# A softmax pipeline over five engines: four probability buffers, every engine's order shifted, five heads with the maximum as bias

## The reference

```python
q = hidden_state @ Wq + bq          # 32 heads of 16
k = encoder_hidden_state @ Wk + bk  # 8 heads of 16
v = encoder_hidden_state @ Wv + bv
scores = jnp.einsum('bkgld,bksd->bkgls', q, k) * scale + mask
attn = jax.nn.softmax(scores, axis=-1)
out = jnp.einsum('bkgls,bksd->bkgld', attn, v)   # then @ Wo + bo, + x, layer norm
```

## Time and profile before

| | |
|---|---|
| median of 3 runs | 2727.72 us |
| the profiled execution | 2733.99 us, span 2732.2 us |
| busy, share of the span | PE 90%, DVE 48%, POOL 33%, ACT 28% |
| mean granted TensorE clock | 0.955 |
| layer 0, first half, PT copy 0 to PT copy 31 | 49.02 to 222.77 us, 173.75 us |
| layer 0, second half, the same | 1410.14 to 1580.55 us, 170.41 us |

### The profile page before, as it was taken

One profiled execution on the slowest core, in us unless ns is written; L12 is line 12 of the kernel. 1 busy time (PEld: TensorE's weight loads), 2 busy tenths in 40 slices (PEclk: granted clock), 3 DMA queues, 4 the chain that ended last, 5 costly groups with the idle time before them and its releaser, 6 DMA issues.

```text
span 2732.2 us, 40539 instructions
## 1 busy us (share of the span) xinstructions
PE 2453.1 (90%) x14896; PEld 2086.6 (76%) x14896; DVE 1322.8 (48%) x2066; ACT 758.7 (28%) x2134; POOL 909.8 (33%) x568
## 2 busy tenths in 40 slices
PE   5776999999799999889966769999998999998898
PEld 4555888888688888767755558888886888886677
DVE  5767433333643333564467783433336333435544
ACT  4553222222222222211145522222222222222111
POOL 4663323222432223322146632322233222323221
PEclk8888999999999999999988889999999999999999
DMA  4001011010110101110130011111002101101000
GB/s 169 9 9 58 33 37 54 31 38 31 66 52 33 38 32 53 37 37 31 62 136 9 9 58 39 46 39 38 31 31 74 47 31 38 52 33 43 31 31 31
DMA packets 34532, 120.08 MB, mean 44 GB/s; under 512 B 3456, under 2 KB 3712, under 8 KB 33408
## 3 DMA queue, kind: packets, MB, share of 16 engines
q1 hardware_dynamic: 34432, 118.69, 12.2%
HBM read 114.48 MB, written 4.19 MB: 43 GB/s over the span
## 4 chain that ended last, share of the span: by engine, by line
PE 76%; DVE 8%; issue 6%; POOL 5%; ACT 2%; DMA 1%; SPq 0%; DVEq 0%; POOLq 0%; ACTq 0%
PE PS L449 63%; PE PS L659 4%; PE PS L641 4%; PE PS L650 2%; PE PS L517 2%; POOL X L316 1%; DVE MX L987 1%; POOL XN L336 1%; DMA BO<-in_bo_rows 1%; DVE XN L982 1%; PE PS L551 1%; DVE X L1006 1%; POOL W L303 1%; POOL XN L329 1%; DVE HF L1081 1%
## 5 line engine op out<-in xcount | busy, mean ns | idle before, releaser
L449 PE MATMUL PS<-AT,W 128*128 128x512 f32 x2496 | 607.5, 395 | 24.9 <-DVE HF L1081 12.1
L449 PEld LDWEIGHTS PS<-AT,W 128*128 128x128 f32 x2496 | 473.1, 190 | 129.7 <-issue 13.4
L1006 DVE TENSOR_TENSOR X<-PS,X 128x512 f32<-128x512 f32 x416 | 284.3, 689 | 334.5 <-PE PS L449 327.2
L390 POOL TENSOR_TENSOR PR<-PR,RC 128x512 f32<-128x512 f32 x128 | 133.6, 1044 | 932.6 <-DVE RC L1171 932.6
L449 PE MATMUL PS<-W,CX 128*128 128x512 f32 x1584 | 397.3, 404 | 34.5 <-DVE Q L974 25.5
L449 PE MATMUL PS<-CT,W 128*128 128x512 f32 x1584 | 399.7, 401 | 30.6 <-DVE W L303 25.7
L449 PE MATMUL PS<-W,CT 128*128 128x256 f32 (+1 forms) x3264 | 412.1, 287 | 0.0
L449 PEld LDWEIGHTS PS<-W,CT 128*128 128x128 f32 x3264 | 401.6, 195 | 0.6
L449 PEld LDWEIGHTS PS<-W,CX 128*128 128x128 f32 x1584 | 294.1, 190 | 105.9 <-DVE Q L974 27.1
L449 PEld LDWEIGHTS PS<-CT,W 128*128 128x128 f32 x1584 | 290.6, 190 | 88.8 <-DVE W L303 26.1
L310 POOL TENSOR_SCALAR W<-RAW 128x1024 fp32r<-128x1024 f32 (+1 forms) x136 | 154.2, 1134 | 554.0 <-PE PS L449 531.7
(11 more groups left out here) (92 smaller groups left out, 2540.5 us busy)
## 6 DMA issues: line engine op xcount, KB each, us to landing
RAW<-in_wq SPq DMA_DIRECT2D x44, 512.0 KB, 4.1
RAW<-in_wo SPq DMA_DIRECT2D x44, 512.0 KB, 3.3
RAW<-in_wk SPq DMA_DIRECT2D x40, 512.0 KB, 3.3
RAW<-in_wv SPq DMA_DIRECT2D x40, 512.0 KB, 3.3
X<-in_x SPq DMA_DIRECT2D x2, 2048.0 KB, 10.0
BVR<-in_bv_rows SPq DMA_DIRECT2D x8, 512.0 KB, 4.2
BIASVR<-in_biasv_rows SPq DMA_DIRECT2D x8, 512.0 KB, 5.7
out<-X SPq DMA_DIRECT2D x4, 1024.0 KB, 4.4
```

The lines of the kernel that those rows point to most:

```text
L390: nc.gpsimd.tensor_tensor(PR[:, :, 0:P], PR[:, :, 0:P], RC[:, 0, 0:BT].unsqueeze(2).to_broadcast([P, BT, P]), ALU.mult).then_inc(norm_done, 1)
L449: ins = nc.tensor.matmul(out, lhs(c, a), rhs(c, b), start=(k == 0), stop=(k == total - 1))
L1006: V_.tensor_tensor(X[:, tile, :], PS[:, bank, :], X[:, tile, :], ALU.add).then_inc(done, 1)
```

## The change

```diff
@@ constants
-OWN = 3
+OWN = 5
+BUFS0 = 4
@@ build: MX, arena and the fourth buffer
-        MX = sb("MX", [P, 3, 8])
+        MX = sb("MX", [P, BUFS0, 8])
...
-        ARENA = 45056
+        ARENA = 49152
...
+        P0D = in_arena("P0D", [P, 1024], F32, 45056)
+
         P0 = [XN[:, 0:2, :].rearrange("p a n -> p (a n)"), XN[:, 2:4, :].rearrange("p a n -> p (a n)"),
-              HF[:].rearrange("p a n -> p (a n)")]
+              HF[:].rearrange("p a n -> p (a n)"), P0D[:]]
@@ gpsimd: order of the turns
                 sub(0)
                 sub(1)
                 norm(0)
+                sub(2)
                 for s in range(STEPS0):
-                    if s + 2 < STEPS0:
-                        sub(s + 2)
                     if s + 1 < STEPS0:
                         norm(s + 1)
+                    if s + 3 < STEPS0:
+                        sub(s + 3)
@@ tensor: order of the turns
                 s0_(1)
                 s0_(2)
+                s0_(3)
                 for s in range(STEPS0):
                     t0(s)
                     if s:
                         pv0(s - 1)
-                    if s + 3 < STEPS0:
-                        s0_(s + 3)
+                    if s + 4 < STEPS0:
+                        s0_(s + 4)
@@ scalar: e0 (the same in sub, norm, t0, soft0 and rec0: s % 3 becomes s % BUFS0)
-                        nc.scalar.activation(P0[s % 3][:, h * P:(h + 1) * P], P0[s % 3][:, h * P:(h + 1) * P], ACT.Exp,
-                                             bias=MX[:, s % 3, h:h + 1], accum_out=SUM0[:, s % 2, h:h + 1])
+                        nc.scalar.activation(P0[s % BUFS0][:, h * P:(h + 1) * P], P0[s % BUFS0][:, h * P:(h + 1) * P], ACT.Exp,
+                                             bias=MX[:, s % BUFS0, h:h + 1], accum_out=SUM0[:, s % 2, h:h + 1])
@@ scalar: order of the turns
                 e0(0)
                 e0(1)
+                e0(2)
                 for s in range(STEPS0):
+                    if s - 1 in Q_AT:
+                        qev0(Q_AT[s - 1])
                     act.wait_ge(t0_ps, s0 + (s + 1))
                     nc.scalar.activation(PT0[s % 2].rearrange("p (a n) -> p a n", a=2), PS[:, BPT:BPT + 2, :],
                                          ACT.Copy).then_inc(t0_ev, 1)
                     if s % 4 == 0 and s:
                         cxhi0(s // 4 - 1)
-                    if s + 2 < STEPS0:
-                        e0(s + 2)
-                    if s - 1 in Q_AT:
-                        qev0(Q_AT[s - 1])
+                    if s + 3 < STEPS0:
+                        e0(s + 3)
@@ vector: when a buffer may be written again
-                    if s >= 3:
-                        dve.wait_ge(t0_ps, s0 + (s - 2))
+                    if s >= BUFS0:
+                        dve.wait_ge(t0_ps, s0 + (s - BUFS0 + 1))
@@ vector: order of the turns
                 soft0(0)
                 soft0(1)
                 rec0(0)
+                soft0(2)
...
                 for s in range(STEPS0):
-                    if s + 2 < STEPS0:
-                        soft0(s + 2)
                     if s + 1 < STEPS0:
                         rec0(s + 1)
+                    if s + 3 < STEPS0:
+                        soft0(s + 3)
@@ kernel
-    nc = bacc.Bacc("TRN2", target_bir_lowering=False, num_devices=1)
+    nc = bacc.Bacc("TRN2", target_bir_lowering=False, num_devices=1, dynamic_dma_scratch_size=2048)
```

More of the change, by code:

```diff
@@ L327, in sub @@
                     pool.wait_ge(max0, hf * STEPS0 + (s + 1))
-                    z = P0[s % 3].rearrange("p (h t) -> p h t", t=P)[:, OWN:KV0, :]
-                    nc.gpsimd.tensor_tensor(z, z, MX[:, s % 3, OWN:KV0].unsqueeze(2).to_broadcast([P, KV0 - OWN, P]),
+                    z = P0[s % BUFS0].rearrange("p (h t) -> p h t", t=P)[:, OWN:KV0, :]
+                    nc.gpsimd.tensor_tensor(z, z, MX[:, s % BUFS0, OWN:KV0].unsqueeze(2).to_broadcast([P, KV0 - OWN, P]),
                                             ALU.add).then_inc(sub0, 1)
@@ L334, in norm @@
                     pool.wait_ge(rc0, hf * STEPS0 + (s + 1))
-                    z = P0[s % 3].rearrange("p (h t) -> p h t", t=P)
+                    z = P0[s % BUFS0].rearrange("p (h t) -> p h t", t=P)
                     nc.gpsimd.tensor_tensor(z, z, RC[:, s % 2, :].unsqueeze(2).to_broadcast([P, KV0, P]),
@@ L517, in t0 @@
                         ins = nc.tensor.transpose(PS[:, BPT + h // 4, h % 4 * P:(h % 4 + 1) * P],
-                                                  P0[s % 3][:, h * P:(h + 1) * P], IDENT[:])
+                                                  P0[s % BUFS0][:, h * P:(h + 1) * P], IDENT[:])
                     ins.then_inc(t0_ps, 1)
@@ L811, in e0 @@
                     for h in range(OWN):
-                        nc.scalar.activation(P0[s % 3][:, h * P:(h + 1) * P], P0[s % 3][:, h * P:(h + 1) * P], ACT.Exp,
-                                             bias=MX[:, s % 3, h:h + 1], accum_out=SUM0[:, s % 2, h:h + 1])
+                        nc.scalar.activation(P0[s % BUFS0][:, h * P:(h + 1) * P], P0[s % BUFS0][:, h * P:(h + 1) * P], ACT.Exp,
+                                             bias=MX[:, s % BUFS0, h:h + 1], accum_out=SUM0[:, s % 2, h:h + 1])
                     act.wait_ge(sub0, s0 + (s + 1))
-                    nc.scalar.activation(P0[s % 3][:, OWN * P:KV0 * P], P0[s % 3][:, OWN * P:KV0 * P], ACT.Exp).then_inc(exp0, 1)
+                    nc.scalar.activation(P0[s % BUFS0][:, OWN * P:KV0 * P], P0[s % BUFS0][:, OWN * P:KV0 * P], ACT.Exp).then_inc(exp0, 1)
                 def cxhi0(u):
@@ L979, in soft0 @@
                     dve.wait_ge(s0_ps, s0 + (s + 1))
-                    if s >= 3:
-                        dve.wait_ge(t0_ps, s0 + (s - 2))
-                    V_.tensor_tensor(P0[s % 3].rearrange("p (i e t) -> p i e t", e=2, t=P),
+                    if s >= BUFS0:
+                        dve.wait_ge(t0_ps, s0 + (s - BUFS0 + 1))
+                    V_.tensor_tensor(P0[s % BUFS0].rearrange("p (i e t) -> p i e t", e=2, t=P),
                                      PS[:, B0:B0 + 4, 0:256].rearrange("p i (e t) -> p i e t", t=P),
@@ L986, in soft0 @@
                     dve.wait_ge(z0, s0 + (s + 1))
-                    V_.tensor_reduce(MX[:, s % 3, :], P0[s % 3].rearrange("p (h t) -> p h t", t=P),
+                    V_.tensor_reduce(MX[:, s % BUFS0, :], P0[s % BUFS0].rearrange("p (h t) -> p h t", t=P),
                                      AXX, ALU.max, negate=True).then_inc(max0, 1)
@@ L991, in rec0 @@
                     dve.wait_ge(exp0, s0 + (s + 1))
-                    V_.tensor_reduce(SUM0[:, s % 2, OWN:KV0], P0[s % 3].rearrange("p (h t) -> p h t", t=P)[:, OWN:KV0, :],
+                    V_.tensor_reduce(SUM0[:, s % 2, OWN:KV0], P0[s % BUFS0].rearrange("p (h t) -> p h t", t=P)[:, OWN:KV0, :],
                                      AXX, ALU.add).then_inc(sum0, 1)
```

## The result

The changed kernel takes 2658.24 us in the median of four runs (2655.48 to 2659.03), against 2727.64 us before. The ratio is 0.9734, 95% interval 0.9717 to 0.9751: 69.4 us faster. The forecast was 2663, the range 2632 to 2704.

The account below looks back on a forecast made before the run. Layer 0 was taken as bound by waits in queue order, not an engine's work. Pieces gave 139 us, 34.7 and 31.4 less per half, minus 0.5 per half at the start: net 65, forecast 2663 us, range 2632 to 2704.

Parts of the forecast that it names:

- (a): ScalarE's eviction of Q ahead of the PT copy: 3.5 us saved at each of six query turns, TensorE late next.
- (b): Fourth buffer and a step more lead in layer 0: the round spans three turns, each turn taken at its longest engine.
- (c): Five own heads: per turn ScalarE +0.6 us, GpSimd's subtraction 0.44 less, VectorE's sum 0.54 instead of 0.809.
- (d): Arena, MX and DMA scratch: no instruction added, taken as 0, bounds -3.5 and +3.5 us.
- Query turns at 5.2 us: Layer 0 turns with a query projection: TensorE's transposes, P*V, scores and projection in a row, 5.2 us at full clock.
- Turns 0 to 7 at GpSimd's 4.13 us: First eight turns of layer 0: GpSimd's norm, subtraction and bias row; with one split and 1 for the start, 37.5 us.
- Plain turns at ScalarE's 3.5 us: Layer 0 turns without projection or output rows: ScalarE's copy, five single exponentials and a joint one, 3.5 us.
- The splits: GpSimd's weight splits in layer 0, 3.4 us each; two in turns 16 to 23 half hidden in idle time, +4.
- the slower one: Rival: low clock holds all of layer 0, TensorE sets the end at 192 us, 2767 us; chance 0.04.
- that of no gain: Rival: norm's semaphore still one turn behind, lead unusable, eviction's 3.5 us lost at out turns, 2728 us; chance 0.03.
- the fully open clock: Rival: clock opens fully and lead covers the splits, layer 0 stage falls to 122 us, 2628 us; chance 0.09.
- The first rival: Query turns and splits keep the pace; four query turns per half cost 9.5 instead of 5.2 us, 2697 us; chance 0.20.

Follow-up runs that it names:

- e1: Kernel before, with only ScalarE's eviction of Q moved ahead of the PT copy: 2694.62 us, ratio 0.9879.
- e5: Changed kernel with Q evicted behind the exponentials again; four buffers, shifted order and five own heads kept: 2707.89 us, ratio 0.9921.
- e7: Kernel before plus a fourth probability buffer (arena and DMA scratch as changed; old order, three own heads, late eviction): 2727.8 us, ratio 0.9995.
- e2: Changed kernel with three own heads and Q evicted behind the exponentials, so four buffers and shifted order alone: 2716.61 us, ratio 0.9953.
- e4: Changed kernel with three own heads instead of five: 2670.4 us, ratio 0.979.
- e6: Changed kernel with three probability buffers instead of four; order, heads and eviction as changed: 2752.23 us, ratio 1.008.
- e3: Kernel before with five own heads instead of three and nothing else: 2738.8 us, ratio 1.0035.
- e12: e8 with GpSimd's last four bias rows in turns 8 to 11 instead of 4 to 7: 2650.77 us, ratio 0.971.
- e8: Changed kernel with GpSimd's split of the output weights after turn 22 instead of 21: 2651.48 us, ratio 0.9709.
- e9: e8 with VectorE's split of the key weights in turn 14 instead of 6: 2658.03 us, ratio 0.9725.

## Why the prediction was right, and where its steps were not

**The bound** (waits in the order of the queues, no full engine): right. The same work now takes 35 us less in each half, and the busy times of the four engines are 105 to 115 us, near the 104 to 114 that the loads gave.

**(a) The eviction** (3.5 us at six query turns, TensorE late next): right, and the largest part. Alone it gives 34 of at most 42 us (e1). There the norm was late next, and not TensorE; with the lead it is TensorE, as forecast, for ScalarE waits 8.7 us for the projection. With the rest in place its absence costs 50 us (e5). The wait went to 4.8 us in three places; that is under 1 us in the mean of six turns, though the longest is 2.2.

**(b) Buffer and lead:** the mechanism was right, the price was never split off. Buffer alone 0 (e7), buffer and order 12 us (e2), with the early eviction 24 us (e1 to e4), order without the buffer a loss of 94 us against the changed kernel (e6). The prediction named the buffer's release and the queue's order as one round, and neither alone opens it. The sign of a wrong step (b), over 20 us of TensorE's waits for norms, did not come: 13.6 us.

**(c) Five heads** (ScalarE has cover): right for the new order, worth 12 us (e4), wrong for the old one, where it costs 10 (e3). VectorE waits for an exponential once in the first half, 2.0 us, where both engines split weights; that sign of a wrong step is there only in this one place. The new durations were 0.544 us for the sum (forecast 0.54), 0.513 for the joint exponential (0.56) and 0.826 for the subtraction (0.81).

**(d) Arena and scratch:** 0, as taken (e7).

**The sum by pieces** gave 139 us, and 138.97 was measured in the first half, but by steps that err both ways:
- *Query turns at 5.2 us* were mis-sized in the first half: 36.2 us for six is 6.0 each. In the second half they are 31.8, 5.3 each. The step counted TensorE's own work and left out that the projection shares PSUM bank BA with the output rows. In turns 12 and 20 it waits 1.94 us for the add, which stands behind the context's low part on VectorE, and these turns take 6.9 us or more. The 4.4 us between the halves lie in turns 0, 8 and 20, where matmuls run at the low level in the first half and not, or less, in the second (twelve in turn 0 take 4.79 us and 3.42); the step had reckoned full speed.
- *Turns 0 to 7 at GpSimd's 4.13 us* is the step that was least right. That GpSimd is the fullest engine there was so: busy 34.51 of 36.41 us. But the copies do not go at its pace. Turns 1 to 3 take 3.24 to 3.34 us, faster than GpSimd's work on a turn (1.90 + 0.83 + 1.28 = 4.0), since its norms have a tile of lead to use up. Turn 6 then pays 7.79 us in one piece where both engines split weights, and VectorE's split stands nowhere in the sum. The 37.5 came out near 36.41 all the same, which is luck in part. e12 shows that another chain is right behind GpSimd's: taking 5.1 us of its work out moves the end by 0.8 and 1.2 us.
- *Plain turns at ScalarE's 3.5 us* were too dear: 3.24 us (58.62 to 61.86, for one). The five single exponentials start 0.39 us apart as assumed. The copy gives way after 0.90 us, where 1.02 was reckoned, and the joint exponential after 0.41, where it was 0.56: each next activation starts before the record of the last one ends.
- *The splits* were half hidden as assumed, but the one after turn 21 was not late for its length alone: it waited 4.30 us for TensorE with a norm queued behind it. The prediction did not name that wait, and e8 takes it away.

**The clock** rose to 0.91, where "near 0.9" was forecast. In the plain turns 1 to 3 transposes are 1.03 to 1.09 us of the 2.3 in which TensorE works, nearly half, and that is the high level. The Trainium skill's remark on transposes (TensorE: Matmul & The Clock Gate, Part 4), which would have kept them low, is not borne out in these turns. The low level came where TensorE had idled: 3.64 us before 152.69, and the transposes there took 1.97. A shorter idle time can end either way. Here is the query projection of turn 20 in the changed kernel, first and second half; the 6 us before the wait are the same work in the same time:

```profile
138.89 4.56 PE L453 MATMUL PS<-AT,W 128*128 128x512 f32 x12 [1.94 <-DVE X L1012]
...
1461.04 3.00 PE L453 MATMUL PS<-AT,W 128*128 128x512 f32 x12 [1.95 <-DVE X L1012]
```

TensorE's matmuls are the same in these kernels but for the twelve in each half named with the result, so its busy time tells how much of a gain is clock. Over the two halves, copy 0 to copy 31, in profiled executions:

| | time, us | TensorE busy | TensorE idle |
|---|---|---|---|
| before | 344.2 | 243.8 | 100.3 |
| e1: early eviction | 308.7 | 234.2 | 74.6 |
| e4: and buffer and order | 286.2 | 226.8 | 59.4 |
| changed kernel: and five heads | 274.9 | 218.2 | 56.7 |

Of the 69.3 us, 25.7 are TensorE's busy time (1.3 of it the scores that moved out) and 43.6 its idle time. The eviction gives 25.8 in idle time and 9.7 in busy time, the lead 15.2 and 7.3, the heads only 2.6 and 8.7. The prediction's sum reckons TensorE at full clock, so this part was in its total; but it priced (a) to (c) by waits and loads alone, and about a third of the gain came by the clock. The ends of matmuls are modelled in the profile, and no run held the clock, so these are readings and not a separation by experiment.

Of the rivals, the slower one (low clock throughout) and that of no gain are out, and the fully open clock too: e8 and e12 come nearest to it, 132 to 135 us a half against its 122. The first rival is right in one part, that query turns stay near 6 us in the first half, and wrong in its price.

## What to carry to other kernels

Look for a short instruction whose input is ready but which stands behind long work for a later tile, and count who waits for it: here a 0.67 us eviction carried half the gain. Depth in a software pipeline needs the order and the buffer together: the buffer alone gave nothing, the order without it (with the early eviction and five heads) lost 22 us against the kernel before, and shifting work to another engine changed its sign with buffer and order. When an instruction waits, ask what is queued behind it; moving one split by a turn gave the fastest pair of versions seen, 2651 us with or without the bias rows moved.

## What the runs showed of the hardware

- VectorE's weight split and GpSimd's elementwise work slow each other down. In the rows of the changed kernel around 75 us GpSimd's norm takes 2.35 us (1.90 elsewhere), its subtraction 1.80 (0.83), VectorE's cast 2.40 (0.94 in e9) and its subtraction 2.80 (1.22 alone in e9). The Trainium skill (SBUF — State Buffer, Terms, "shared port pair") says that the two engines arbitrate for a port pair exclusively and the loser blocks. The rows agree: VectorE's subtraction ends at 79.80, 1.08 us after the end of GpSimd's norm at 78.72, and GpSimd's subtraction ends at 80.48, 0.68 after that, each near its duration alone. VectorE's bias and maximum, with one SBUF input, kept 1.22 us beside GpSimd's norms.
- The granted clock can differ behind the same wait in the same program: 1.94 us of idle time in TensorE, then twelve matmuls in 4.56 us in one half and in 3.00 in the other. Such a turn costs 1.55 us more, so small differences between single profiled executions are to be read turn by turn.
- Taking the overlap of the two splits away gained 1 us there and lost 2 where the split then stood (e9).
